# A DLRM interaction tower on one core: scaling in PSUM, sums by VectorE, products by Pool

## The reference, cut to what matters

```python
e = stack([tbl_m[ids[:, m]] for m in range(40)], axis=1)   # (512, 40, 16)
x = e
for k in (k0, k1, k2):          # (128,40,40), (128,128,40), (128,128,40)
    x = einsum('bhd,bmd,ohm->bod', x, e, k)
    outputs.append(sum(x, axis=-1))
h = concatenate(outputs + [dense_ctx], axis=1)             # (512, 400)
h = maximum(h @ W_top1 + b_top1, 0)
h = maximum(h @ W_top2 + b_top2, 0)
y = h @ W_top3                                             # (512, 1)
```

## Time and profile before

| | us |
|---|---|
| median of 3 runs | 758.27 |
| lowest and highest | 753.87, 759.46 |
| the profiled execution, own time | 760.51 |
| its span, first to last instruction | 758.6 |
| mean granted TensorE clock | 0.978 |

### The profile page before, as it was taken

One profiled execution on the slowest core, in us unless ns is written; L12 is line 12 of the kernel. 1 busy time (PEld: TensorE's weight loads), 2 busy tenths in 40 slices (PEclk: granted clock), 3 DMA queues, 4 the chain that ended last, 5 costly groups with the idle time before them and its releaser, 6 DMA issues.

```text
span 758.6 us, 12855 instructions
## 1 busy us (share of the span) xinstructions
PE 678.7 (89%) x2558; PEld 471.8 (62%) x2558; DVE 674.9 (89%) x1542; ACT 523.9 (69%) x1753; POOL 517.8 (68%) x443
## 2 busy tenths in 40 slices
PE   0478999999979989899899899898989999998998
PEld 0256667676655757576667667575757676774483
DVE  2559999999979999999799999999999999989291
ACT  1257777777666868777767768686777777887293
POOL 6457796878758697978678787969687875572000
PEclk9999999999989999999989999999999999997699
DMA  6451212222120212121211203131212111100000
GB/s 199 129 196 40 75 42 65 53 51 65 14 77 29 82 33 73 43 73 43 62 42 23 93 18 86 28 85 30 74 42 75 43 47 66 46 1 29 0 1 1
DMA packets 56679, 43.08 MB, mean 57 GB/s; under 512 B 37007, under 2 KB 40335, under 8 KB 56352
## 3 DMA queue, kind: packets, MB, share of 16 engines
q1 hardware_dynamic: 51488, 41.08, 17.9%
q0 software_dynamic: 5120, 1.32, 1.8%
HBM read 40.41 MB, written 1.97 MB: 56 GB/s over the span
## 4 chain that ended last, share of the span: by engine, by line
PE 37%; DVE 27%; issue 17%; DMA 6%; POOL 6%; SPq 3%; ACT 2%; DVEq 2%; ACTq 0%; POOLq 0%
DVE chain L426 13%; PE Y L507 8%; DVE chain L391 8%; PE Y L509 7%; PE Y L508 7%; DVE pairs L358 3%; POOL x0g L219 3%; PE X L478 3%; DMA pairs<-scratch 3%; POOL fold L256 3%; DVE pairs_lo L365 2%; SPq L187 2%; ACT scaled L317 2%; DMA scratch<-x0g 2%; DMA x0g<-in_table,rows_now 1%
## 5 line engine op out<-in xcount | busy, mean ns | idle before, releaser
L317 ACT ACTIVATE scaled<-Y,xtok 128x128 f32<-128x128 f32 x1536 | 421.9, 380 | 128.1 <-PE Y L509 110.0
L507 PE MATMUL Y<-k1lo,x1hi 128*128 128x512 f32 x640 | 293.0, 458 | 22.8 <-DVE chain L426 21.2
L509 PE MATMUL Y<-k1hi,x1lo 128*128 128x512 f32 x640 | 254.6, 398 | 0.0
L508 PE MATMUL Y<-k1hi,x1hi 128*128 128x512 f32 x640 | 253.8, 397 | 0.0
L219 POOL DMA_INDIRECT x0g<-in_table,rows_now x160 | 197.7, 1236 | 42.1 <-issue 37.5
L426 DVE SCALAR_TENSOR_TENSOR chain<-Y,xtok,chain 128x128 f32<-128x128 f32 x768 | 211.4, 337 | 5.0 <-PE Y L509 4.8
L256 POOL TENSOR_TENSOR fold<-fold,scaled 128x512 f32<-128x512 f32 x128 | 173.8, 1358 | 28.3 <-ACT scaled L317 18.1
L507 PEld LDWEIGHTS Y<-k1lo,x1hi 128*128 128x128 f32 x640 | 121.1, 189 | 91.0 <-DVE chain L426 51.8
L256 POOL TENSOR_TENSOR fold<-scaled 128x512 f32<-128x512 f32 x64 | 90.7, 1417 | 87.3 <-ACT scaled L317 63.4
L508 PEld LDWEIGHTS Y<-k1hi,x1hi 128*128 128x128 f32 x640 | 121.5, 190 | 38.8 <-issue 14.6
L509 PEld LDWEIGHTS Y<-k1hi,x1lo 128*128 128x128 f32 x640 | 121.2, 189 | 29.7
(11 more groups left out here) (77 smaller groups left out, 468.2 us busy)
## 6 DMA issues: line engine op xcount, KB each, us to landing
pairs<-scratch SPq DMA_DIRECT2D x112, 240.0 KB
A<-scratch SPq DMA_DIRECT2D x16, 240.0 KB
k1raw<-in_k SPq DMA_DIRECT2D x1, 2560.0 KB, 10.3
x0g<-in_table,rows_now POOLq DMA_INDIRECT x160, 2.7
k2s<-in_k SPq DMA_DIRECT2D x1, 2560.0 KB, 9.2
scratch<-x0g SPq DMA_DIRECT2D x96, 20.0 KB, 1.7
pairs<-in_w SPq DMA_DIRECT2D x3, 256.0 KB, 2.8
w2s<-in_w SPq DMA_DIRECT2D x1, 512.0 KB, 3.9
```

The source lines that it names most:

```text
L317: ins = nc.scalar.activation(scaled[:, rank(c) - 1, i * O:(i + 1) * O], Y[(NCH * tile + c) % YB][:, i * O:(i + 1) * O], ACT.Copy, scale=xt ...
L507: nc.tensor.matmul(y, hi[:, tok], k1lo[:, cols], start=True, stop=False)
L508: nc.tensor.matmul(y, hi[:, tok], k1hi[:, cols], start=False, stop=False)
L509: nc.tensor.matmul(y, lo[:, tok], k1hi[:, cols], start=False, stop=True).then_inc(s_y, 1)
```

## The change

- `OWNER = "ADAADAAADA"`: seven chunks for ACT, three for VectorE. ACT writes its scaled chunk back into the Y bank, in place (chunk 0 goes to an SBUF tile, `first`). VectorE adds it from there to `chain` (`add_scaled`, `last_sum`), and the last addition writes into the bank of chunk 9. One reduction sums the four quarters of that bank to x2 (`add_quarters`). Pool's folds and VectorE's merges are gone.
- Order on VectorE in a tile: sum9 of the tile before, mac1, quarters of the tile before, sum2, mac4, (x1lo in tile 3), sum3, sum5, sum6, (z0 in tile 3), mac8, sum7. Each waits for the step before it that it builds on.
- Pool multiplies the rolls with A (`product`): three in tile 0, three in tile 1, one in tile 2, ahead of the tile's gathers, three, three and four. In the head VectorE does it.
- Layer 0 is all float32: seven products of two rows each, at chunks 5, 9, 13, 17, 20, 23 and 26 of the group; no split. The transposes come after chunk 1, in the bank X1; xtok after chunk 3; x1hi after chunk 28; G after chunk 5 and its copy after chunk 6.
- Six Y banks in place of five; seven `pairs` buffers in place of four, so a roll waits only for layer 0 of the group before.
- The head: 20 extra matmuls on TensorE (their result is not used); stores and rolls of group 0 are issued half by SP, half by ACT; k2s is issued by SP behind its four rolls; k1hi and k1lo are mixed with them.
- w2s has a place of its own and is loaded without a wait; h1, H and the buffers of layer 2 move.

The core of the diff:

```diff
-YB = 5
-OWNER = "ADAADAADAD"
+YB = 6
+OWNER = "ADAADAAADA"
+XTOK_PE_AT, XTOK_AT = 1, 3
+L0_AT = (5, 9, 13, 17, 20, 23, 26)
+X1HI_AT = 28
+X1LO_TILE, Z0_TILE = 3, 3
+G_AT, GCOPY_AT = 5, 6
+PRODUCTS_OF_TILE = ((0, 1, 2), (3, 4, 5), (6,), ())
+GATHERS_OF_TILE = ((0, 3), (3, 6), (6, 10), (0, 0))
...
+            for r in range(0, ROLLS // GF, 2):
+                store_copy(sp, 0, r)
+            sp.wait_ge(s_scratch, 16 * (ROLLS // GF))
+            sp.dma_start(A3[0][0:PR, :], rolled_rows(0, 0, 0)).then_inc(s_a3, 16)
+            for c in range(0, NC0, 2):
+                load_roll(sp, 0, c)
             sp.dma_start(k2s[:, :, :], k2.rearrange("h (m o) -> h m o", o=O)).then_inc(s_k2, 16)
...
-                    for a in range(2, NA - EXTRA):
-                        pool.wait_ge(s_yA, NA * (T + 1) + a + 1)
-                        if a > 2:
-                            pool.wait_ge(s_fold, FOLDS * (T + 1) + a - 2)
-                        nc.gpsimd.tensor_tensor(sums[:, :], scaled[:, 1, :] if a == 2 else sums[:, :],
-                                                scaled[:, a, :], ALU.add).then_inc(s_fold, 1)
+                        for c in PRODUCTS_OF_TILE[j]:
+                            product(u, slot, c)
...
-                                ins = nc.scalar.activation(
-                                    scaled[:, rank(c) - 1, i * O:(i + 1) * O],
-                                    Y[(NCH * tile + c) % YB][:, i * O:(i + 1) * O], ACT.Copy,
-                                    scale=xtok[slot % 2][:, j, m:m + 1])
+                                ins = nc.scalar.activation(first[:, o] if c == 0 else y[:, o], y[:, o], ACT.Copy,
+                                                           scale=xtok[slot % 2][:, j, m:m + 1])
...
+            def last_sum(T, tile):
+                y = Y[bank_of(NCH * tile + NCH - 1)]
+                dve.wait_ge(s_yA, act_count(T, NCH - 1))
+                dve.wait_ge(s_chain, chain_count(T, "sum7"))
+                nc.vector.tensor_tensor(y[:, :], chain[tile % 2][:, :], y[:, :], ALU.add).then_inc(s_chain, 1)
+            def add_quarters(T, tile, ready):
+                y = Y[bank_of(NCH * tile + NCH - 1)]
+                dve.wait_ge(s_chain, ready)
+                nc.vector.tensor_reduce(x2[tile % 2][:, :], y[:, :].rearrange("p (m o) -> p o m", o=O), AX.X,
+                                        ALU.add).then_inc(s_chain, 1)
...
+                        def add_scaled(c, after):
+                            y = Y[bank_of(NCH * tile + c)]
+                            dve.wait_ge(s_yA, act_count(T, c))
+                            dve.wait_ge(s_chain, after)
+                            nc.vector.tensor_tensor(sums[:, :], sums[:, :], y[:, :], ALU.add).then_inc(s_chain, 1)
+                        last_sum(T - 1, before)
+                        dve.wait_ge(s_xtok, g + 1)
+                        dve.wait_ge(s_yA, act_count(T, 0))
+                        mac(1, chain_count(T - 1, "sum9_of_previous"))
+                        add_quarters(T - 1, before, chain_count(T, "sum9_of_previous"))
+                        add_scaled(2, chain_count(T, "mac1"))
+                        mac(4, chain_count(T, "sum2"))
...
+            def wait_for_bank(u, k):
+                f = previous_in_bank(k)
+                T, c = u * (GPB * TPG) + f // NCH, f % NCH
+                if c == 0:
+                    pe.wait_ge(s_yA, act_count(T, 0))
+                elif c == NCH - 1:
+                    pe.wait_ge(s_chain, chain_count(T + 1, "quarters_of_previous"))
+                else:
+                    pe.wait_ge(s_chain, chain_count(T, f"mac{c}" if OWNER[c] == "D" else f"sum{c}"))
+            pe.wait_ge(s_k1hi, 4)
+            for i in range(WARM):
+                nc.tensor.matmul(Y[i % 2][:, :], k1hi[:, 0:P], k1hi[:, 0:BANK], start=True, stop=True)
...
+                            if p == XTOK_PE_AT:
+                                pe.wait_ge(s_a3, 16 * (g + 2))
+                                pe.wait_ge(s_x1free, g + 1)
+                                transposes(g + 1, (slot + 1) % 2)
```

More of the change, by code:

```diff
@@ L53, in prep_steps @@
-def prep_steps():
-    names = ["xtok"]
-    for kind, n in (("prod", NC0), ("ph", NS), ("pl", NS), ("l0_", NC0)):
-        names += [f"{kind}{c}" for c in range(n)]
-    names += X1_LAG
-    return sorted(names, key=position)
+WARM = 20
+XTOK_PE_AT, XTOK_AT = 1, 3
[5 more added lines that the diff above has]
+GATHERS_OF_TILE = ((0, 3), (3, 6), (6, 10), (0, 0))
+STEPS = ("sum9_of_previous", "mac1", "mac1", "mac1", "mac1", "quarters_of_previous", "sum2",
+         "mac4", "mac4", "mac4", "mac4", "sum3", "sum5", "sum6", "mac8", "mac8", "mac8", "mac8", "sum7")
@@ L239, in body @@
                     T = u * (GPB * TPG) + tile
-                    gathers = not last or slot < GPB - 2
-                    if gathers and j == 0:
-                        pool.wait_ge(s_prod, NC0 * (u * GPB + slot + 1))
-                        take_rows(u * GPB + slot + 2, slot % 2)
                     pool.wait_ge(s_xtok, u * GPB + slot + 1)
@@ L404, in _, with k1_low @@
+            def k1_low(c):
                 dve.wait_ge(s_k1hi, c + 1)
@@ new lines, in body @@
+                        last_sum(T - 1, before)
[5 more added lines that the diff above has]
+                        mac(4, chain_count(T, "sum2"))
+                        if j == X1LO_TILE and (not last or slot < GPB - 1):
+                            x1_low(g + 1, (slot + 1) % 2)
@@ L436, in _ @@
+                        add_scaled(3, chain_count(T, "mac4"))
+                        add_scaled(5, chain_count(T, "sum3"))
+                        add_scaled(6, chain_count(T, "sum5"))
+                        if j == Z0_TILE and (not last or slot < GPB - 1):
+                            z0_sums(g + 1)
+                        mac(8, chain_count(T, "sum6"))
+                        add_scaled(7, chain_count(T, "mac8"))
             over_groups(dve, body)
-            for k in range(MERGE):
-                merge(NTILES - 1, (NTILES - 1) % 2, k)
```

400 lines of the change are left out of this document (163 added, 237 removed).

## The result

| | before | after |
|---|---|---|
| median, us | 757.38 (16 runs) | 747.97 (16 runs) |
| lowest and highest | 750.45, 761.38 | 741.29, 751.68 |
| span of the profiled execution | 758.6 | 748.7 |
| mean granted TensorE clock | 0.978 | 0.975 |

The ratio is 0.9901, with a 95% interval of 0.9873 to 0.9928: the change gains 1.0%, and 742 forecast 2.1%. 748 lies inside the range of 724 to 764. The direction was right, the size twice what came. The ratios in this document leave out executions more than 1.5% above the fastest of their kernel, the medians do not, which matters for e3 (three of ten runs), e5 (one of six) and e10 (two of six), whose profiles are of such an execution.

The account below looks back on a forecast made before the run. Bound: Pool's work slowing the other engines. Groups 14 x 1.54 = 21.6, loop end less 1.5, less 3.2, plus 0.4, head less 1.1: 16.2 us off 760.5 profiled, 758.27 median; forecast 742 (own range 730 to 752; 724 to 764 also given).

Parts of the forecast that it names:

- Group period: Regular group of four tiles: 38.8 us against 40.34, from steps of 10.1, 10.1, 9.45 and 9.15.
- the ring: Chunk 5 waits for the bank of the previous tile's sum9, free after mac1 and quarters: 8.6 us round, TensorE alone 7.55.
- VectorE's adds and ACT in place: Per tile: VectorE's adds from PSUM take 0.60, or 0.71 with a wait, uncontended; ACT scales a chunk in 1.07 us.
- Rival 3: ACT is slower in place in PSUM; at 1.52 us a chunk, 44.7 a group and 837 us; chance 0.10.
- rival 2: The ring has more hand-overs, 1.5 us a group: 40.3 a group, 759 to 763 us; chance 0.14.
- Pool's part at no cost: In each group Pool swaps 12 folds for seven products, 6.8 us less work, hidden by its lead: cost 0.
- The 12.4 us are stalls: Stalls mostly where the loop body starts again, 12.4 us over 15 groups, were taken as unchanged.
- 1.1 us lost: Head: TensorE stops behind chunk 1 until about 43.5, waiting for A; 1.1 us lost, bounds 5 gained, 4 lost.
- for the last stores: Head: 1.5 us for group 1's last stores after 39, then 3 for A.
- rival 4: The head gains: A of group 1 isn't late, 5 us instead of -1.1, giving 736; chance 0.09.
- The end of the loop: Gatherless group goes from 37.27 to 38.8, last group's tiles from 7.54 to 8.6; the end is 0.4 shorter.
- The tail, 0: After the loop: TensorE still idles about 3 us before the last G product, what follows is the same; change 0.

Follow-up runs that it names:

- e3: The kernel before, with the k2s load issued behind the loop instead of behind the rolls of group 0: 752.95 us, ratio 0.9904.
- e5: The changed kernel with k2s issued behind the loop and the quarters sum ahead of the first scale-and-adds: 729.20 us, ratio 0.9626.
- e10: The changed kernel with k2s behind the loop, the quarters sum earlier and bank numbers continuing over the body edge: 724.68 us, ratio 0.9544.
- e2: The changed kernel with VectorE's quarters sum put ahead of the four scale-and-adds (mac1): 735.93 us, ratio 0.9727.
- e12: The changed kernel with five Y banks in place of six: 764.74 us, ratio 1.0118.
- e7: The changed kernel with six of ACT's seven scaled chunks written to SBUF instead of in place to PSUM: 792.17 us, ratio 1.0474.
- e11: The changed kernel with layer-0 products back on VectorE and Pool's row numbers ahead of its diagonal: 756.30 us, ratio 1.0015.
- e9: The changed kernel with only the bank numbering changed, so that it continues over the body edge: 745.63 us, ratio 0.9868.
- e1: The changed kernel with the k2s load issued behind the loop instead of behind SP's rolls of group 0: 741.84 us, ratio 0.9814.
- e4: The changed kernel without the 20 extra warm matmuls of the head: 748.74 us, ratio 0.99.
- e6: The changed kernel with all four loop bodies written out, no loop on any engine: 745.63 us, ratio 0.9859.

## Why the prediction was half right

**Group period: right.** 38.8 forecast, 38.85 measured, and with the structure named: TensorE's own work from tile 0 to 1 and from 1 to 2, the ring into tile 3, VectorE's work from there to tile 0. All four steps came within 0.14 us of their forecast (10.24, 10.12, 9.38 and 9.11), so the sum is no cancelling of errors. e2 removed the ring and uncovered the floor of 37.8 (37.99 measured), e12 lengthened it by one chunk.

**VectorE's adds and ACT in place: right.** 0.686 us against 0.68 for undisturbed operations of this width, by e7 for the reason given. ACT's four scalings in place take 1.11 or 1.12 us in the rows of the regular groups, 367 ns each. That PSUM is the quicker destination, the rule in the Trainium skill's "ScalarE: Activation LUTs" ("Step-by-step: what each stage is for"), agrees in sign: 367 ns against 380 before and 397 in e7. It moved no tile off its forecast; only part of the ring is ACT's. Rival 3 fell with it, and rival 2 too: the ring has no more hand-overs than counted.

**Pool's part at no cost: right as far as it goes.** The move to Pool costs the path nothing, but its worth was never priced. By e11, with its second difference, it is 15 us up to the last z0 sum and 8.3 in the medians, nearly all that the change gains in the end.

**"The 12.4 us are stalls ... I leave them as they are, since the new body has the same shape": wrong.** This step cost some 2.6 of the 6.3 us missing. The shape was the same, the number of banks wasn't. The three edges cost 14.2 us over a regular group where they had cost 9.8. The short reuse of four chunks is 4.5 of that (1.5 an edge), and with it came 1.0 of lower clock; what e9 leaves is 8.7, 1.1 below the 9.8. Against this, smaller stalls of the kernel before are gone, 1.9 us that the prediction had kept too: two groups of 41.35 and one of 40.73, less two of 39.09 now. The line to read was `bank_of`, against the 160 chunks of a body; nothing in the trace of before could show it, since five divides 160.

**The head, "1.1 us lost": mis-sized.** Where and why TensorE stops was right, behind the second chunk, for A of group 1 behind k2s. Its end was put at 43.5 and came at 46.68. The term that failed is the 1.5 us "for the last stores". The stores of group 1 were put at 39 and issued at 38.18, once gathers that Pool had issued long before had landed. But from there to the issue of A it took 5.2 us (43.39), not 1.5; A then took 3.3, against the 3 of the forecast. The stores' issue alone is 2.82 us, and even without k2s, in e1, the way from the first store to A is 4.2 us (32.98 to 37.14). The 1.0 above that fits the pace, which was taken too fast as well: by the sum of 4.5 MB k2s would have landed at 39, some 14 us after its issue, and it took 16.8, until 42.0. And layer 1 began 2.0 us earlier, not 5, and the warm matmuls gave nothing of it (e4). The head came out some 3 us worse than forecast (the second z0 sum at 85.45, against 82.89 before plus 1.1 less 1.5 = 82.5), at the end of the first group; e1 is rival 4, A early, come true by an edit that the change didn't contain.

**The end of the loop: right in size, wrong in one reason.** 8.6 was forecast for the last group's tiles, from the ring; G products come 8.69 apart (649.84, 658.53, 667.22). But there VectorE runs without a gap, so it is a bound, beside the ring:
```profile
657.59 0.68 DVE L392 TENSOR_TENSOR chain<-chain,Y 128x512 f32<-128x512 f32 x1
658.37 1.13 DVE L384 SCALAR_TENSOR_TENSOR chain<-Y,xtok,chain 128x128 f32<-128x128 f32 x4
```
Between 657.59 and the dependent step lie 0.78 us; inside the loop, the same pair stands 0.72 apart (319.30 to 320.02). Dependent steps of VectorE cost some 0.07 more in the written-out body. This fits e6, all of whose groups take 39.09 instead of 38.85, and e2, which gained nothing in the last group.

**The tail, 0: right for the two profiled executions, by luck.** It lost the 2.7 of the last group and nothing else: from the last G product to the end it is 65.87 us before and 65.85 after. But both had the lower clock for long; in e11 and e12 the same stretch takes 57.7 and 57.6. What I had not seen is that the time behind the last z0 sum changes from execution to execution, from 96.51 (e11) to 106.09 us (e4), by far more than the 2.7.

**Sum.** 16.2 us forecast, 9.9 measured between the profiled executions. Of the 6.3 between them, 3 are the head, by the end of the first group, and 3.3 lie from there to the last z0 sum (0.7 for 14 groups at 0.05, the rest is the 2.6 of stalls).

## What to carry to other kernels

When a ring of buffers gets a new length, divide the loop's count by it: a remainder is paid at each pass through the loop's edge, and no trace of the old length shows it. Where a ring of waits is the bound, look at what stands between the releasing result and its consumer in program order; one reduction moved ahead of four independent instructions was worth 12 us. And a large load that nobody needs for long goes behind the small ones that somebody waits for, even if its queue is idle at that moment: it holds back the gathers of another queue (e1: the stores behind them go out 5.2 us earlier without it).

## What the runs showed of the hardware

- With the scaled chunks in PSUM and not in SBUF (changed kernel against e7), VectorE's adds take 686 ns instead of 918, and with them get shorter Pool's products (1287 against 1534), Pool's gather instructions (961 against 1106) and ACT's own writes (367 against 397). I had not expected it of the gathers.
- The same sequence of dependent VectorE instructions runs 0.07 us per step slower in code written out than in the loop (0.78 against 0.72). Why is open: the waits there compare with constants, in the loop with a register, and no run separates the two.
- A load of 2.5 MB that took 9.2 us in one kernel took 16.8 in the other, beside the small stores and loads of the head. In e1, without it, the stores of group 1 could be issued 5.2 us earlier.
- What a pause of TensorE costs is not fixed. In e9, after 3.10 us of idleness (209.27) the matmuls came at the higher clock at once, and after 3.08 at the same place one loop pass later (367.80) they were 0.43 us apart instead of 0.235. After 3.4 us before the last G product the lower clock held for some 4 us in e12 and some 20 in the changed kernel (granted clock 0.50 up to 702, 0.79 in the next 4 us). The spread between executions of the changed kernel goes with it, 741.29 us at a mean clock of 0.986 to 751.68 at 0.975; so a difference of a few us between two kernels is read at its place in the trace first, and from a median of six runs only then. It also makes that pause a thing to remove; no run here tried it.
